# A graph-attention layer on one core: steps of two slots, an accumulator written last, x gathered earlier and a closing stage on plain loads

## The reference

```python
q = (x @ Wq.T + bq).reshape(N, 32, 8) * 32 ** -0.5
k = (x @ Wk.T + bk).reshape(N, 32, 8)
v = (x @ Wv.T + bv).reshape(N, 32, 8)
s = einsum('edh,edh->eh', q[src], k[dst])
e = exp(s - segment_max(s, src)[src])
attn = e / segment_sum(e, src)[src]
out = segment_sum(attn[:, None, :] * v[dst], src)
x = layernorm(x + out.reshape(N, -1) @ Wo.T + bo)
```

## Time and profile before

| | |
|---|---|
| runs | 4096.47 us median of 3 (4023.46 to 4236.0) |
| profiled execution | 4017.71 us, span 4015.6 us |
| busy share of the span | DVE 80%, POOL 61%, PE 55%, PEld 38%, ACT 37% |
| mean granted TensorE clock | 0.743 of full speed |
| moved by DMA | 665.86 MB, mean 166 GB/s |
| from issue to landing, medians | q gather (line 492) 3.1 us, `store_q` (line 434) 1.9 us |
| stages, by their first instructions | prepare to 1112, setting up to 1261, main loop to 3723, closing to the end |

### The profile page before, as it was taken

One profiled execution on the slowest core, in us unless ns is written; L12 is line 12 of the kernel. 1 busy time (PEld: TensorE's weight loads), 2 busy tenths in 40 slices (PEclk: granted clock), 3 DMA queues, 4 the chain that ended last, 5 costly groups with the idle time before them and its releaser, 6 DMA issues. The chain is left out here.

```text
span 4015.6 us, 59591 instructions
## 1 busy us (share of the span) xinstructions
PE 2227.2 (55%) x7109; PEld 1514.8 (38%) x7109; DVE 3211.0 (80%) x8164; ACT 1504.6 (37%) x6480; POOL 2447.6 (61%) x2365
## 2 busy tenths in 40 slices
PE   3999888653002555555555545555555555544776
PEld 3788775432001333333333333333333333323443
DVE  8554467799223999999999999999999999977776
ACT  0110002221001555555555555555555555534332
POOL 3221120003767777777777777777777777765677
PEclk9966568776555788778777787777877778766777
DMA  1211013226513788878887887888777788799222
GB/s 33 64 58 32 16 43 101 89 67 125 171 36 96 231 233 232 232 232 232 231 232 232 232 232 231 232 232 231 232 232 231 232 232 232 229 177 169 80 92 85
DMA packets 329217, 665.86 MB, mean 166 GB/s; under 512 B 63462, under 2 KB 191750, under 8 KB 329016
## 3 DMA queue, kind: packets, MB, share of 16 engines
q0 software_dynamic: 160768, 518.27, 46.4%
q1 hardware_dynamic: 168392, 146.96, 12.7%
HBM read 599.35 MB, written 65.86 MB: 166 GB/s over the span
## 5 line engine op out<-in xcount | busy, mean ns | idle before, releaser
L931 POOL DMA_INDIRECT kv<-kv_rows,idx x1794 | 1863.0, 1038 | 583.7 <-issue 538.5
L1032 PE MATMUL sum_ps<-pv,ident 128*128 128x264 f32 x2392 | 902.0, 512 | 1299.3 <-DVE pv L825 1299.3
L1032 PEld LDWEIGHTS sum_ps<-pv,ident 128*128 128x128 f32 x2392 | 511.3, 237 | 1712.1 <-DVE pv L825 1393.1
L987 ACT ACTIVATE pv<-kv,s 128x33 f32<-128x33 f32 x4784 | 1084.4, 309 | 53.9 <-ACT s L977 27.3
L790 DVE TENSOR_TENSOR prod<-kv,q 128x768 f32<-128x768 f32 x598 | 569.2, 952 | 59.7 <-DMA kv<-kv_rows,idx 59.6
L797 DVE TENSOR_REDUCE s<-prod 128x24 f32<-128x768 f32 x598 | 565.5, 946 | 0.0
L977 ACT ACTIVATE s<-s 128x32 f32<-128x32 f32 x598 | 137.0, 229 | 1126.1 <-DVE s L818 1126.1
L1034 PE MATMUL sum_ps<-pv,ident 128*128 128x264 f32 x1196 | 497.3, 508 | 0.0
L507 PE MATMUL hist_ps<-hot_lo,hot_hi 125*98 125x128 bf16 x1600 | 372.1, 409 | 121.7 <-DVE hot_hi L174 121.7
L825 DVE TENSOR_TENSOR pv<-kv,s 128x528 f32<-128x528 f32 x598 | 417.4, 698 | 0.3 <-ACT s L977 0.3
L507 PEld LDWEIGHTS hist_ps<-hot_lo,hot_hi 125*98 125x98 bf16 x1600 | 370.3, 259 | 123.2 <-issue 68.7
(11 more groups left out here) (164 smaller groups left out, 2450.5 us busy)
## 6 DMA issues: line engine op xcount, KB each, us to landing
q<-q_perm SPq DMA_DIRECT2D x598, 128.0 KB, 3.7
kv<-kv_rows,idx POOLq DMA_INDIRECT x1794, 4.0
kv_rows<-kv_st SPq DMA_DIRECT2D x98, 260.0 KB, 3.0
xt_sb<-in_xT SPq DMA_DIRECT2D x98, 128.0 KB, 3.2
node_rows<-q_st SPq DMA_DIRECT2D x98, 128.0 KB, 3.4
q_perm<-kv_st SPq DMA_DIRECT2D x98, 128.0 KB, 1.9
kv_st<-node_rows,node_id POOLq DMA_INDIRECT x98, 3.1
cols<-edge_keys,run_at POOLq DMA_INDIRECT x98, 2.5
```

What stands on the lines that cost most here:

```text
L931: pool.indirect_dma_start(out=kv[:, j, g, :], out_offset=None, in_=kv_rows, in_offset=bass.IndirectOffsetOnAxis(ap=idx[:, j, g:g + 1], axi ...
L987: last = act.activation(pv[:, b, V * VW + at_h:V * VW + at_h + HD + 1], kv[:, j, V, D + at_h:D + at_h + HD + 1], ACT.Copy, scale=s[:, b, V ...
L1032: pe.matmul(sum_ps[b][:, 0:VW], ident[:, :], pv[:, b, g * VW:(g + 1) * VW], start=g == 0, stop=False)
```

## The change

- G becomes 2, C 40, U and B (the steps written out in one pass of the loop) 8. STEPS becomes 40 / 2 + (1562 + 97) / 2 = 849.
- `scale_acc` and `add_sum` go. In their place DVE writes the scaled accumulator as one more slot of `pv` (`carry`, at the end of a step), PE adds it as the last matmul of the step's sum, and ACT copies the finished sum from PSUM into the accumulator (`store`, after six of the eight heads of the next step). `carry` of step k + 1 waits for the `store` of step k. ACT reads the tile of each step with a table look-up of its own. ACT's index copy moves behind the weighing.
- POOL gathers x in tile order into SBUF as soon as `node_id` is there (98 gathers), ahead of the q gathers; SP stores it to `x_perm` in one DMA, ahead of all `store_q`. The starts and the sorted keys are stored from ACT's queue instead of SP's.
- Closing: SP loads x with plain loads; buffers of 4; ACT copies the transposed tile and normalises (Identity with a scale and a shift per row); DVE computes the shift instead.

```diff
-G = 3
+G = 2
-C = 39
+C = 40
-U = 6
+U = 8
-B = 6
+BEFORE_STORE = 6
+B = 8
...
+                sp.wait_ge(x_got, 16 * TILES)
+                sp.dma_start(x_perm.rearrange("(t p) d -> p t d", p=P), x_all).then_inc(x_out, 16)
...
                 pool.wait_ge(nodes_ready, 1)
+                for t in range(TILES):
+                    pool.indirect_dma_start(out=x_all[:, t, :], out_offset=None, in_=x_rows,
+                                            in_offset=bass.IndirectOffsetOnAxis(ap=node_id[:, t:t + 1], axis=0),
+                                            bounds_check=NP - 1, oob_is_err=False).then_inc(x_got, 16)
...
                 stage_bodies(0, sum(EARLY) + MIDDLE)
+                act.wait_ge(starts_ready, 1)
+                act.dma_start(node_rows[:, D:D + 1].rearrange("(p f) one -> p (f one)", f=P),
+                              start_i[0:TILES, :].bitcast(F32), allow_slow_non_contiguous=True).then_inc(starts_out, 16)
...
-                def scale_acc(k, b, tile, first=False):
-
+                def carry(k, b, tile, first=False):
                     if not first:
-                        dve.wait_ge(acc_added, k)
...
+                        dve.wait_ge(acc_stored, k)
+                    dve.tensor_tensor(pv[:, b, G * VW:].rearrange("p (h w) -> p h w", w=HD + 1),
+                                      acc[:, bass.ds(tile * VW, VW)].rearrange("p (h w) -> p h w", w=HD + 1),
+                                      s[:, b, G * HEADS:].unsqueeze(2).to_broadcast([P, HEADS, HD + 1]), ALU.mult).then_inc(carry_made, 1)
...
                     score_sum(k + 1, b1, peeled=peel and j == 0)
+                    look_up(k + 2)
+                    old_maximum(k + 1, b1, tile1, peeled=peel and j == 0)
+                    mask_scores(k + 1, b1, col1)
                     weigh(k, j % U, b, peeled=peel and j < 2)
...
                     maxima(k + 1, b1, tile1)
-                    if before is not None:
-                        add_sum(k - 1, b1, before)
                     if not last:
                         score(k + 2, (j + 2) % U, turn + (j + 2) // U)
-                    scale_acc(k, b, tile, first=peel and j == 0)
+                    decode(b)
                     differences(k + 1, b1, tile1)
...
+                    carry(k, b, tile, first=peel and j == 0)
...
+                    weigh_heads(j, b, range(0, BEFORE_STORE))
+                    if stored:
+                        store(k - 1, 1 - b)
+                    weigh_heads(j, b, range(BEFORE_STORE, HEADS)).then_inc(last_made, 1)
+
+                def store(k, b):
+
+                    v = act.value_load(step_tab[0:1, bass.ds(k, 1)], min_val=0, max_val=TAB * C * P - 1)
+                    tile = bounded(act, v & (P - 1), TILES)
+                    act.wait_ge(summed, k + 1)
+                    act.activation(acc[:, bass.ds(tile * VW, VW)], sum_ps[b][:, 0:VW], ACT.Copy).then_inc(acc_stored, 1)
...
                         k = kk * B + j
-                        indices(k + U, j % U, kk * (B // U) + j // U + 1)
                         weights(k + 1, (j + 1) % 2)
                         weigh_last(k + 1, (j + 1) % U, kk * (B // U) + (j + 1) // U, (j + 1) % 2)
+                        indices(k + U, j % U, kk * (B // U) + j // U + 1)
...
                     pe.wait_ge(last_made, k + 1)
-                    pe.matmul(sum_ps[b][:, 0:VW], ident[:, :], pv[:, b, V * VW:G * VW], start=False, stop=True).then_inc(summed, 1)
...
+                    pe.matmul(sum_ps[b][:, 0:VW], ident[:, :], pv[:, b, V * VW:G * VW], start=False, stop=False)
+                    pe.wait_ge(carry_made, k + 1)
+                    pe.matmul(sum_ps[b][:, 0:VW], ident[:, :], pv[:, b, G * VW:], start=False, stop=True).then_inc(summed, 1)
...
+                def stage(t, h, first=False):
+                    act.wait_ge(oT_made, t + 1)
+                    if not first:
+                        act.wait_ge(proj_made, t - 1)
+                    act.activation(oT[:, h, :], oT_ps[h][:, 0:D], ACT.Copy).then_inc(oT_staged, 1)
...
+                def normalise(t, j, turn):
+                    act.wait_ge(shift_made, t + 1)
+                    if not isinstance(t, int) or t >= W:
+                        act.wait_ge(out_done[j], 16 * turn)
+                    act.activation(res[:, j, :], y[:, j, :], ACT.Identity, bias=shift[:, j, :], scale=rstd[:, j, :]).then_inc(res_made, 1)
...
+                    sp.dma_start(x[:, j, :], x_perm[bass.ds(t * P, P), :]).then_inc(x_in[j], 16)
```

More of the change, by code:

```diff
@@ L893, in _ @@
                 weigh(k, k % U, k % 2)
[L894 to L898, removed]
+                carry(k, k % 2, bounded(dve, tile_r[k % 2], TILES))
+                for r in tile_r + col_r + [entry_r]:
                     dve.free_register(r)
@@ new lines, in at_tile @@
+                def at_tile(t, j, turn):
+                    inside = not isinstance(t, int)
+                    j1 = (j - 1) % W
+                    if inside or 0 <= t + 3 < TILES:
+                        clear_of_zero(t + 3, (j + 1) % 2, counted=t if inside or t >= 1 else None)
+                    elif 1 <= t <= TILES:
+                        dve.wait_ge(stats_made, t)
+                    if inside or 1 <= t <= TILES:
+                        aggregate(t - 1, j1)
+                    if inside or 0 <= t < TILES:
+                        add_x(t, j, turn, first=not inside and t < W)
+                    if inside or 1 <= t <= TILES:
+                        scale(t - 1, j1)
+                    if inside or 0 <= t + 3 < TILES:
+                        invert(t + 3, (j + 1) % 2)
@@ L1118, in at_tile @@
-                    if inside or 0 <= t < TILES:
-                        dve.wait_ge(eps_set, 1)
-                        dve.wait_ge(stats_made, t + 1)
-                        dve.bn_aggr(mv[:, h, :], stats[:, h, :]).then_inc(mv_made, 1)
+                        divide(t + 3, (j + 1) % 2, first=not inside and t + 3 < 2)
                 dve.memset(eps_sb[:, :], EPS).then_inc(eps_set, 1)
-                bodies = (TILES - 3) // 4
-                for t in range(-3, 4):
-                    at_tile(t, t % 2, t // 2)
+                bodies = (TILES - 3) // W
@@ L1133, in _, with turn @@
             @block.tensor
             def _(pe):
-                def turn(t, h):
+                def turn(t, h, first=False):
                     pe.wait_ge(o_made, t + 1)
+                    if not first:
+                        pe.wait_ge(oT_staged, t - 1)
                     for kc in range(2):
@@ new lines, in _ @@
+                act.wait_ge(eps_set, 1)
+                stage(0, 0, first=True)
+                stage(1, 1, first=True)
+                stage(2, 0)
+                for t in range(W):
+                    deviation(t, t)
+                    stage(t + 3, (t + 1) % 2)
+                    normalise(t, t, 0)
+                bodies = (TILES - 3) // W
+                with act.Fori(1, bodies) as i:
+                    for j in range(W):
+                        deviation(i * W + j, j)
+                        stage(i * W + j + 3, (j + 1) % 2)
+                        normalise(i * W + j, j, i)
@@ new lines, in _, with load_x @@
+                for t in range(bodies * W, TILES):
+                    deviation(t, t % W)
+                    if t + 3 < TILES:
+                        stage(t + 3, (t + 1) % 2)
+                    normalise(t, t % W, t // W)
+            @block.sync
+            def _(sp):
+                def load_x(t, j, first=False):
+                    if not first:
+                        sp.wait_ge(y_made, t - W + 1)
+                    sp.dma_start(x[:, j, :], x_perm[bass.ds(t * P, P), :]).then_inc(x_in[j], 16)
+                for j in range(W):
+                    load_x(j, j, first=True)
+                with sp.Fori(1, TILES // W) as i:
+                    for j in range(W):
+                        load_x(i * W + j, j)
+                for t in range(TILES // W * W, TILES):
+                    load_x(t, t % W)
@@ L1194 @@
+                for j in range(W):
+                    pool.wait_ge(out_done[j], 16 * len(range(j, TILES, W)))
 def kernel(x, src, dst, L0_gnn_Wq, L0_gnn_bq, L0_gnn_Wk, L0_gnn_bk, L0_gnn_Wv, L0_gnn_bv, L0_gnn_Wo, L0_gnn_bo):
```

235 lines of the change are left out of this document (115 added, 120 removed).

## The result

The new kernel takes 3832.35 us, median of four runs (3821.02 to 3837.23), against 4061.38 of before in the runs beside it (4023.46 to 4236.0). Single executions of one kernel can run some per cent slower than its others; the ratio 0.9517, with an interval of 0.9488 to 0.9547, compares only the undisturbed ones. The profiled execution took 3836.62, span 3834.8.

What follows compares the result with a forecast made beforehand. POOL, which never rests, was taken to bound the main loop. From 4015.6, idle steps -67, real steps -6, prepare +33 and closing -65 gave 3910.6, with 2.1 around the span 3913 us; range 3830 to 4075.

Steps and rivals of the forecast that it cites:

- Real steps: Main loop: 559 steps at 4.01 us (2242) become 813 at 2.75 (2236), -6 us (-55 to +99).
- 0.03 of jitter: Main loop: us per real step added to POOL's 2.72, giving 2.75.
- clock mixture: Main loop: PE's granted clock kept at a mean of 0.79, upper level 58% of the time, sums 2.22 us a step.
- rival 1: Main loop: PE takes POOL's place at the low clock, 2.88 us a step, +105, 4018 us; chance 0.20.
- rival 2: Main loop: ACT becomes the bound with one table look-up uncovered, 3.03 us a step, 4140 us; chance 0.14.
- Idle steps: Main loop: DMA-bound idle steps become 36, 124 us instead of 191, -67 us.
- Prepare: Prepare stage: the x store ahead of every store_q makes POOL stop at the ninth q gather; +33 us.
- Rivals 3 and 5: Prepare: sort delays x gathers, 32 us later, chance 0.06; x store delays nothing, 30 us less, shares forecast's 0.55.
- The bound of +60: Prepare stage: upper bound of the added us, if x is moved at the loop's 232 GB/s.
- Closing: Closing: 2.2 us a tile, DVE plus the root's trip with PE partly low, 226 against 291, -65 (-118 to -26).
- rival 4: Closing: ACT changes tables between root and copy, 3.7 us a tile, stage 373 instead of 226, 4060 us; chance 0.05.
- The 2.72: Main loop: POOL's us per step, two gathers at 1.30, plus 0.09, plus the loop's turn 0.21 / 8.

Runs made afterwards that it cites:

- two_psum_operand: New kernel (steps of two) with the second operand of DVE's score, weigh and carry taken from a PSUM bank of ones; 3731.56 us.
- loop_only: Kernel before with the new main loop alone, prepare and closing being those of before; 3913.01 us.
- steps_of_three: New kernel with G back at 3 (C 39, U and B 6), the carry, x and closing kept; 4147.83 us.
- normalised_by_dve: New kernel with the last normalise step back on DVE, in place of the shift on DVE and the Identity on ACT; 3864.08 us.
- x_gathered_in_closing: New kernel without the early x gathers and x store; POOL gathers x in the closing, four tiles ahead; 3894.86 us.
- two_slots_old_sum: Kernel before with only G = 2 (C 40, U and B 8); DVE still scales the accumulator and adds the sum; 4697.18 us.

## Why the prediction was right, point by point

The direction, and the places where time was gained and lost, were right; the size was not. The span fell by 181 where I had 105, and the range holds the result by 2 us. Of the 76 missing, 47 are the closing, 22 the real steps, 4 the idle steps, and 4 the end of the loop, while the prepare stage cost 1 more.

*Real steps.* POOL's own rows were the right measure: from the first real gather to the first idle one it is 2216.7 against 2244.9, -28 where I had -6, because I added 0.03 of jitter that isn't there. The gathers are 1.363 apart and not the 1.30 that I gave as the sign. The clock mixture which I carried over from the earlier trace rows didn't hold, so the condition of rival 1 never arose: PE's sums (two matmul instructions) took 0.71 or less in the timeline, at a granted clock of 0.99. DVE (2.65 costed, 2.52 with POOL out of the way) and ACT (2.55 costed, 2.39 busy) were slightly dear. ACT's two look-ups are covered, so rival 2 is out; its timeline has no pause before the `store` or before the index copy:

```profile
2002.17 0.37 ACT L1012 ACTIVATE acc<-sum_ps 128x264 f32 x1
2002.44 0.52 ACT L992 ACTIVATE pv<-kv,s 128x33 f32<-128x33 f32 x2
2002.87 0.19 ACT L982 ACTIVATE idx<-cols 128x2 int32 x1
```

I wrote that no named wait would show. Some do, of 0.3 (DVE's `pv` 69.8 us in 1900), but they are POOL's usual issue time under another name.

*Idle steps.* 124 against 195, -71 for -67: each of the two costs was within 4 us (191 and 124). The spread rows show that the one row was the cause. That DMA's share sets the pace is less clear: in other kernels with these idle steps it was 0.82 (`two_psum_operand`) to 1.00 (`loop_only`) at the same 1.67 to 1.68 a gather.

*The rest of the loop*, 103 - 28 - 71 = 4, lies between the last gather and the closing (23.2 before, 19.3 after); I had not costed it.

*Prepare.* The gap and its place were right, and so was the end: 1001 for 998 at the ninth gather. Rivals 3 and 5 fall: the x gathers took 1.05 on average and ran from 825.7 to 957.0, 131 us as costed, and the store held the q rows for 31 us. One step was right by luck, by two errors: I pushed the first q gather by 3 (it was 6) because I took the starts' earlier store as covered. It was worth 18, and the x gathers cost 25. The bound of +60 was a slip: 12.85 MB at 232 GB/s are 55 us, 17 more than 38, so +50.

*Closing.* The mis-sized term: 2.2 us a tile, where 1.65 was measured. I had computed DVE's 1.66 from the earlier trace rows and then added a trip over the root and PE at the low clock. The trip doesn't show (DVE is busy 94%), and the granted clock was 1.00. That the four buffers and the work of three tiles in between cover the trip is how I read the program; fewer buffers were not tried. POOL gone from the chain carries most of it, as the prediction had it. There is no table switch, so rival 4 is out, and no load per pass either, which I had costed: one load serves the stage.

*The rule that I set aside.* "0.025 us at the median" of the earlier trace rows was the wrong reading. A hold strikes only the gathers that begin inside a long DVE product, so it stands in the mean and the maximum. I had it in front of me twice, as the third gather's 0.09 and as the "loop's turn" of 0.21 in the earlier trace rows. The 2.72 came out because holds of about that size go on in the new loop, not because the two causes I gave were right: the number was luck. `steps_of_three` shows that the same loop can meet the holds otherwise and lose 275 us.

What stays open is what sets the phase in which DVE meets the gathers. That a meeting more or less is the whole difference, the traces show: what the gathers of 1500 to 3400 take over 1.00 adds up to 82 us in the new kernel, 99 with x in pieces and 102 with the idle rows spread, and to 44 and 43 in the two kernels without `score` on two SBUF operands. But three more runs have the same loop and no edit in it or in the idle steps: `loop_only`, `normalised_by_dve` and `x_gathered_in_closing`, with 89, 92 and 95 us, and 1.366 to 1.374 a gather over the real steps. So the new kernel's profile is the lowest of six. The scatter of the runs fits that too (16 to 27 us in the three kernels with `score` on two SBUF operands that ran four times, 4 and 7 in the two without). Each kernel has one profile, and they were not all taken on one chip; whether the edits or the execution set the phase was not tried.

## What to carry to other kernels

Cost a loop by the engine that shows no named wait, and look at the spread of its instructions' durations, not at their median: here a tail of 1.3 to 1.7 over a floor of 1.0 was another engine holding it. Removing slack elsewhere may change when two engines meet, so a saving ahead of such a loop can vanish inside it: take the encounter out first (here an operand in PSUM), then the stalls. And where a stage has several tiles in flight, as this closing has, cost it by its busiest engine first: here 1.66 a tile for DVE against 1.65 measured, while the round trip that I added on top was the error.

## What the runs showed of the hardware

- A gather on POOL that began while a DVE product with two SBUF operands ran ended 0.87 us after that product (all 304 that took over 1.02 us between 1500 and 3400 in the new kernel: 0.867 to 0.884; all 474 such in the kernel before: 0.866 to 0.885). Those that began in its last 0.13 us kept to 1.00 to 1.02, and so did some that began in its first 0.05. With the second operand in PSUM a gather took 0.99 to 1.02, wherever it began.
- The granted TensorE clock was 0.50, the lower level, all through the loop of `two_slots_old_sum` (two sums in 3.70 us), 0.79 before (three in 4.01), 0.99 after (three in 2.73).
- Root, copy and Identity alternating on ACT took one table load of 1.28 us in the whole closing.
- 128 reads of one row: a gather cost 1.75 us with DMA at 0.99 in the new kernel; over different rows 1.40 with DMA at 0.79.
